# A graph layer over a dense adjacency: banks on 2048-byte starts, residual rows bank by bank, the emptying split, the first tiles rounded in parts, engine programs without loops

## What is computed

```python
h_in = jnp.maximum(_layernorm(x, axis=-1), 0.0)        # x is 10000 x 128
h = item_feat @ W_item.T + b_item                      # 10000 x 128
b = h_in @ W_user.T + b_user                           # 10000 x 128
return x + jax.nn.relu(adj @ h + b)                    # adj is 10000 x 10000
```

## Time and profile before

| | |
|---|---|
| median of three runs | 1132.15 us |
| the profiled execution | 1133.93 us |
| its span, first to last instruction | 1132.4 us |
| PE busy, matmuls | 1113.5 us, 98% |
| DVE busy | 974.1 us, 86% |
| ACT busy | 765.4 us, 68% |
| POOL busy | 23.0 us, 2% |
| DMA traffic | 421.44 MB, mean 372 GB/s |
| chain that ended last | PE 84%, DVE 6%, DMA 5% |

### The profile page before, as it was taken

How to read it: one execution, slowest core, us unless ns; L and a number is a source line. 1 busy time by engine, 2 the same in 40 slices (tenths; PEclk the granted TensorE clock), 3 DMA queues, 4 the chain that set the end, 5 groups by cost and what they waited for, 6 DMA issues and landing times.

```text
span 1132.4 us, 13599 instructions
## 1 busy us (share of the span) xinstructions
PE 1113.5 (98%) x4998; PEld 914.9 (81%) x4998; DVE 974.1 (86%) x683; ACT 765.4 (68%) x482; POOL 23.0 (2%) x47
## 2 busy tenths in 40 slices
PE   5999999999999999999999999999999999999998
PEld 4888888888888888878878888888788887887887
DVE  5899988889999878888988889888888898988887
ACT  4766766666666666676666666666666776666664
POOL 0000000001000000000000001000000010000000
PEclk9999999999999999999999999999999999999999
DMA  9999989999999999999999999999999999999994
GB/s 356 396 408 384 368 331 369 366 358 379 414 387 377 360 369 379 369 392 409 388 367 361 365 381 381 399 402 382 355 355 378 386 372 404 401 380 354 350 391 161
DMA packets 63378, 421.44 MB, mean 372 GB/s; under 512 B 7725, under 2 KB 9205, under 8 KB 63329
## 3 DMA queue, kind: packets, MB, share of 16 engines
q1 hardware_dynamic: 59984, 406.38, 92.6%
q0 software_dynamic: 3344, 14.34, 3.6%
HBM read 415.57 MB, written 5.12 MB: 372 GB/s over the span
## 4 chain that ended last, share of the span: by engine, by line
PE 84%; DVE 6%; DMA 5%; issue 3%; ACT 1%; SPq 1%; DVEq 0%; ACTq 0%
PE acc L536 27%; PE acc L529 27%; PE acc L531 26%; DMA a_ring<-in_adj_tiles 4%; DVE lo_ring L346 4%; ACT hi_ring L286 1%; PE acc L500 1%; PE acc L472 1%; DVE y L407 1%; PE acc L493 1%; DMA items<-in_item_t 1%; SPq L199 1%; PE acc L509 0%; SPq L192 0%; DVE stat L366 0%
## 5 line engine op out<-in xcount | busy, mean ns | idle before, releaser
L346 DVE TENSOR_TENSOR lo_ring<-a_ring,hi_ring 128x2000 fp32r<-128x2000 f32 x390 | 868.9, 2240 | 136.2 <-ACT hi_ring L286 135.8
L286 ACT CAST hi_ring<-a_ring 128x2000 fp32r<-128x2000 f32 x390 | 728.8, 1869 | 350.0 <-PE acc L536 324.0
L529 PE MATMUL acc<-hi_ring,h_lo 128*128 128x500 f32 x1560 | 617.9, 396 | 0.0
L536 PE MATMUL acc<-lo_ring,h_hi 128*128 128x500 f32 x1560 | 607.4, 389 | 3.9 <-DVE lo_ring L346 3.9
L531 PE MATMUL acc<-hi_ring,h_hi 128*128 128x500 f32 x1560 | 604.6, 388 | 0.0
L536 PEld LDWEIGHTS acc<-lo_ring,h_hi 128*128 128x128 f32 x1560 | 293.3, 188 | 67.8 <-DVE lo_ring L346 8.3
L529 PEld LDWEIGHTS acc<-hi_ring,h_lo 128*128 128x128 f32 x1560 | 293.5, 188 | 64.4 <-issue 8.5
L531 PEld LDWEIGHTS acc<-hi_ring,h_hi 128*128 128x128 f32 x1560 | 293.4, 188 | 62.0 <-issue 4.6
L472 PE MATMUL acc<-wi,items 128*128 128x128 f32 x156 | 23.9, 294 | 11.7 <-DMA items<-in_item_t 9.9
L472 PEld LDWEIGHTS acc<-wi,items 128*128 128x128 f32 x156 | 23.0, 206 | 13.9 <-issue 7.5
L351 DVE TENSOR_TENSOR h_full<-acc,bi 128x384 f32<-128x384 f32 x26 | 14.3, 552 | 11.5 <-PE acc L472 11.5
(11 more groups left out here) (27 smaller groups left out, 83.2 us busy)
## 6 DMA issues: line engine op xcount, KB each, us to landing
a_ring<-in_adj_tiles SPq DMA_DIRECT2D x390, 1000.0 KB, 7.0
rows<-in_x_rows POOLq DMA_DIRECT2D x20, 250.0 KB, 7.2
y<-in_x_t POOLq DMA_DIRECT2D x5, 1000.0 KB, 10.4
items<-in_item_t SPq DMA_DIRECT2D x12, 384.0 KB, 8.1
out_t<-y POOLq DMA_DIRECT2D x16, 250.0 KB, 5.5
out_t<-y SPq DMA_DIRECT2D x4, 250.0 KB, 2.1
a_rem<-in_adj_rem SPq DMA_DIRECT2D x20, 31.2 KB, 9.3
items<-in_item_t SPq DMA_DIRECT2D x2, 192.0 KB, 5.8
```

What stands on the lines that cost most here:

```text
L286: nc.scalar.copy(hi_ring[:, r, :], a_ring[:, s, 0:GROUP_W]).then_inc(hi_written, 1)
L346: nc.vector.tensor_tensor(lo_ring[:, r, :], a_ring[:, s, 0:GROUP_W], hi_ring[:, r, :], ALU.subtract).then_inc(lo_written[s], 1)
L529: nc.tensor.matmul(acc[k][:, 0:BANK_W], h_lo[:, c, :], hi_ring[:, r, cols], start=(c == 0), stop=False, skip_group_check=True)
L536: last = nc.tensor.matmul(acc[k][:, 0:BANK_W], h_hi[:, c, :], lo_ring[:, r, cols], start=False, stop=(c == CHUNKS - 1), skip_group_check=True)
```

## The change

- `hi_ring` and `lo_ring` get a pitch of 512 elements (2048 bytes) a bank. They are allocated early, behind three small tensors and a gap of 96 elements, so that the rings themselves begin on a multiple of 2048 bytes. `a_ring` now has banks of 500 and a slot of 2000 elements. In HBM the layout is as before.
- The x columns are loaded bank by bank, 0.25 MB each, the first when 9 tiles of a group are rounded and one more every 12.
- Emptying: two banks after the second tile of the next group, two after the third.
- The first three tiles are rounded and subtracted in four parts each. The first tile is loaded in four parts as well.
- `wi` and `bi` are loaded by ACT's queue. Only one trio of h stands ahead of the first tile; the next ones are made at tiles 1, 3 and 4. The first row load waits for two rounded tiles.
- PE makes 8 small products of the identity before the first trio and 6 behind it, into a bank that nobody reads.
- All loops of engines are written out, and waits on counts of zero fall away.

```diff
-        a_ring = sb("a_ring", [P, A_SLOTS, PITCH])
-        hi_ring = sb("hi_ring", [P, S_SLOTS, GROUP_W], F32R)
-        lo_ring = sb("lo_ring", [P, S_SLOTS, GROUP_W], F32R)
+        sb("gap", [P, RING_GAP])
+
+        hi_ring = sb("hi_ring", [P, S_SLOTS, ACC_BANKS, BANK_PITCH], F32R)
+        lo_ring = sb("lo_ring", [P, S_SLOTS, ACC_BANKS, BANK_PITCH], F32R)
...
+        a_ring = sb("a_ring", [P, A_SLOTS, ACC_BANKS, BANK_W])
...
-            sp.dma_start(wi[:, :], w_item_t).then_inc(w_item_loaded, 16)
             sp.dma_start(items[:, 0, 0:TRIO_W], item_t[:, 0:TRIO_W]).then_inc(item_first_loaded, 16)
-            sp.dma_start(bi[:, :], b_item_rows).then_inc(bias_loaded, 16)
-            load_tile(FREE, 0, 0)
+            for k in range(ACC_BANKS):
+                cols = slice(k * BANK_W, (k + 1) * BANK_W)
+                landed = part_loaded[k] if k < PARTS else a_loaded[0]
+                sp.dma_start(a_ring[:, 0, k, :], adj_tiles[0, :, cols]).then_inc(landed, 16)
             sp.dma_start(items[:, 0, TRIO_W:PIECE_W], item_t[:, TRIO_W:PIECE_W]).then_inc(item_loaded[0], 16)
-            load_tile(FREE, 1, 1)
+            load_tile(0, 1)
+            load_tile(0, 2)
             load_piece(1)
...
-            def load_x(g):
-                pool.dma_start(y[:, 0:GROUP_W], x_t[bass.ds(g, 1), :, :].rearrange("o p n -> (o p) n")).then_inc(x_loaded, 16)
+            def load_x(g, k):
+                pool.dma_start(y[:, k, :], x_t[g, :, k, :]).then_inc(x_loaded, 16)
+
+            pool.wait_ge(hi_written, 2)
+            load_rows(0, 0)
+            for g in range(GROUPS):
+                if g > 0:
+                    for k in range(ACC_BANKS):
+                        pool.wait_ge(y_ready[k], g)
+                        pool.dma_start(out_t[g - 1, :, k, :], y[:, k, :]).then_inc(stored, 16)
+
+                    pool.wait_ge(stored, g * (16 * ACC_BANKS))
+                for k in range(UNITS):
+                    if (g, k) != (GROUPS - 1, UNITS - 1):
+
+                        pool.wait_ge(centred_ready, g * UNITS + k + 1)
+                        load_rows(*divmod(g * UNITS + k + 1, UNITS))
+
+                    pool.wait_ge(hi_written, g * CHUNKS + X_AT + k * BODY)
+                    load_x(g, k)
...
+            def round_part(c, k):
+                s, r = c % A_SLOTS, c % S_SLOTS
+                if c == 0 and k < PARTS:
+                    act.wait_ge(part_loaded[k], 16)
+                else:
+                    tile_there(0, c)
+                nc.scalar.copy(hi_ring[:, r, k, 0:BANK_W], a_ring[:, s, k, :]).then_inc(part_hi if k < PARTS else hi_written, 1)
...
+                    elif c == AHEAD - 1:
+                        empty(g - 1, 0)
+                        empty(g - 1, 1)
+                    elif c == AHEAD:
+                        empty(g - 1, 2)
+                        empty(g - 1, 3)
...
+            pe.wait_ge(ident_set, 1)
+            warm(WARM_FIRST)
+            pe.wait_ge(w_item_loaded, 16)
+            h_trio(0)
+            warm(WARM_THEN)
```

More of the change, by code:

```diff
@@ L82 @@
 VAR_AT = 8
+X_AT = 9
 SQRT_AT = 11
@@ L88, with unit_at @@
 AHEAD = 2
-VECTOR_LOOP_AT = 2
-SCALAR_LOOP_AT = 6
+def unit_at(c, at):
+    k, rest = divmod(c - at, BODY)
+    return k if rest == 0 and 0 <= k < UNITS else None
 def graph_layer(nc, adj_tiles, adj_rem, ones_row, item_t, x_rows, x_t, w_item_t, b_item_rows, w_user_t, b_user, out_t):
@@ L142, in graph_layer @@
         a_loaded = [sem(f"a_loaded{s}") for s in range(A_SLOTS)]
+        part_loaded = [sem(f"part_loaded{k}") for k in range(PARTS)]
+        part_hi = sem("part_hi")
+        part_lo = sem("part_lo")
         rem_loaded = sem("rem_loaded")
@@ L274, in _ @@
         @block.scalar
         def _(act):
[L277 to L286 removed]
+            act.dma_start(wi[:, :], w_item_t).then_inc(w_item_loaded, 16)
@@ L332, in _, with h_rem_round, square @@
-            for g in range(1, GROUPS - 1):
-                group(g)
-                for c in range(AHEAD):
-                    round_hi(g + 1, c)
-            group(GROUPS - 1)
+            def h_rem_round():
+                act.wait_ge(h_rem_summed, 1)
+                for k in range(ACC_BANKS):
+                    row = k * ROWS_BLOCK
+                    nc.scalar.copy(h_rem[row:row + REM, :], h_full_rem[:, :]).then_inc(rem_set, 1)
+            def square(g, k):
+                act.wait_ge(centred_ready, g * UNITS + k + 1)
+                nc.scalar.activation(squares[:, :, :], centred[:, :, :], ACT.Square).then_inc(squares_ready, 1)
@@ L457, in _, with warm @@
+            for k in range(ACC_BANKS):
+                empty(GROUPS - 1, k)
         @block.tensor
         def _(pe):
+            def warm(times):
+                for _ in range(times):
+                    nc.tensor.matmul(warm_bank[0:ROW_T, 0:ROW_T], ident[:, :], ident[:, :], start=True, stop=True, skip_group_check=True)
             def h_trio(trio):
@@ L543, in _, with h_rem_product, turn_normed @@
-            pe.wait_ge(w_item_loaded, 16)
-            for trio in range(LEAD):
-                h_trio(trio)
-            pe.wait_ge(ident_set, 1)
-            for g in range(GROUPS):
-                group(g)
+            def h_rem_product():
+                pe.wait_ge(item_rem_loaded, 16)
+                nc.tensor.matmul(h_rem_bank[0:REM, 0:HID], items_rem[:, :], wi[:, :],
+                                 start=True, stop=True, skip_group_check=True).then_inc(h_rem_done, 1)
+            def turn_normed(g, k):
+                turned, n = turned_of(g), ROW_T
+                if g > 0 and k == 0:
+                    pe.wait_ge(y_ready[0], g)
+                pe.wait_ge(normed_ready, g * UNITS + k + 1)
+                for t in range(ROW_TILES):
+                    last = nc.tensor.transpose(turned[:, t * n:(t + 1) * n], normed[:, t, :], ident[:, :])
+                last.then_inc(turned_ready, 1)
```

437 lines of the change are left out of this document (214 added, 223 removed).

## The result

The changed kernel takes 1124.54 us (median of four runs, 1123.56 to 1124.76) where the kernel before, timed beside it, takes 1132.62 (1131.33 to 1133.58): a ratio of 0.9928, 95% interval 0.9911 to 0.9945. So it is faster by 8.1 us, inside the range and on the side that was forecast, but by only half of the 16 us. The profiled executions, 1133.93 and 1124.51 us, are 9.4 us apart, their spans 9.7.

A forecast was written before the change was run, and what follows sets the result against it. PE's matmul spacing was taken to bound nearly all the time. Start 3, residual rows 4.7, emptying 1.8 and bank alignment 7 made 16.5 us, less 0.5: 1132 - 16 = 1116 us, range 1070 to 1132.

The forecast's parts named there:

- What bounds the kernel: Whole kernel: the spacing of PE's matmul starts, 225.8 ns, bounds nearly all the time; DVE, ACT and DMA have slack.
- Start, 3 us: First tiles: fewer h products ahead and a row load moved let tile 3's third matmul start 3 us earlier.
- The two signs named: Expected in the changed kernel's trace: first main matmul near 9 us, tile 3's low part near 23.
- The lower bound, 1 us: Start of the kernel: the gain would be only 1 us if landings slip by 2 us.
- Warm-up, splitting, no loops, each 0: Identity products on PE, three tiles rounded in parts, and written-out engine loops were each to gain 0.
- Residual rows bank by bank, 4.7 us: Loads of x: 0.25 MB pieces remove PE waits for the low part in four places, 4.7 us, at least 2.
- Emptying split, 1.8 us: Four group boundaries: two banks emptied later let DVE's subtract begin 1.2 us sooner, removing waits of 1.8 us.
- Banks on 2048 bytes, 7 us: Moving operands of tile matmuls: aligned starts give every tile the better slot's 2.69 us instead of 2.71, 7 us.
- The second: Rival: the address cost each matmul up to 15 ns; spacing falls to 211 to 221 ns, 1053 to 1100 us; 24%.
- The third: Rival: equal bank starts make operand reads collide, 4 ns more a matmul, 1142 us; slower from 2 ns; 12%.
- The fourth: Rival: landings bind the start, another DVE step replaces the emptying, small x loads slow the queue; 1126 to 1132 us; 18%.

The follow-up runs named there:

- norm_later_0: Changed kernel with the layer norm steps and x loads of group 0 nine tiles later; 1122.11 us, ratio 0.9906.
- no_warm: Changed kernel without its 14 small products of the identity on PE; 1124.37 us, ratio 0.9927.
- align_unrolled: Kernel before with rings and banks aligned to 2048 bytes and the loops of SP, POOL, ACT and DVE written out; 1132.23 us, ratio 0.9996.
- split_six: Changed kernel with six tiles instead of three rounded and subtracted in parts; 1124.26 us, ratio 0.9931.
- x_at_once: Changed kernel with x loaded as one 1 MB DMA a group at its old place; 1129.51 us, ratio 0.9964.
- norm_later_1: Changed kernel with all layer norm steps of groups 1 to 4 two tiles later; 1123.23 us, ratio 0.9919.
- packed: Changed kernel with banks at 2000 bytes again and the rings' start modulo 2048 as in the kernel before; 1129.33 us, ratio 0.9963.
- align_layout: Kernel before with the changed kernel's whole SBUF layout, but its own loops, order, x load and emptying; 1129.94 us, ratio 0.9970.
- align_only: Kernel before with only hi_ring and lo_ring changed: banks 2048 bytes apart, rings on a multiple of 2048; 1132.40 us, ratio 0.9993.
- rings_behind: Changed kernel with a_ring allocated ahead of the gap and rings, banks still on multiples of 2048 bytes; 1126.85 us, ratio 0.9953.
- a_ring_pitch: Changed kernel with a slot of a_ring at 2048 elements instead of 2000; 1126.03 us, ratio 0.9944.

## Why the prediction missed by half

The side, the range and the kinds of gain came out; the sum did not. The steps that failed are three of its terms. The start and the residual rows were added up although both are bound by the same landings: up to tile 78 they were to give 3 and 1.8 us and gave 1.3. The emptying was checked one tile ahead only: 0.4 instead of 1.8. And the spacing was taken from the better slot for all tiles: 4.9 instead of 7.

**What bounds the kernel**: right. PE's starts account for the whole difference.

**Start, 3 us**: 1.4. The two signs named came, tile 0 near 9 (8.09) and tile 3's low part near 23 (21.50). The step stopped at tile 3. It said that tiles cannot be had before they land, and then credited the gain at tile 3 as if the later tiles were not landing-bound as well; tile 6 landed at 28.3 in both. The lower bound, 1 us, was the better value, though not for the reason given there, late landings: tile 3 landed at 17.3, where the step had 19.0. `norm_later_0` shows what else lay behind it: without the layer norm's centring ahead of tile 5's subtract, tile 6 starts 2.1 us earlier, while it lands only 0.3 us earlier.

**Warm-up, splitting, no loops, each 0**: right for the warm-up and the loops (`no_warm`, `align_unrolled`). More splitting brings nothing (`split_six`); the first three split tiles were not undone alone.

**Residual rows bank by bank, 4.7 us**: about 2.9 of it came, the share of groups 1 to 4. The 1.8 us of group 0 hardly did: the wait at tile 13 is nearly as long as in the earlier trace rows, although of x only a quarter was loaded by then (issued at 35.90, landed at 42.71 us) and tile 13 itself landed at 49.5 instead of 51.1. PE was earlier by as much and met the same wait, for a late landing with the layer norm's steps on DVE on top. So the split load did act in group 0, but what it gave was the start's gain over again: `x_at_once` loses that gain by tile 78. Two terms of the sum were one. `norm_later_0` takes the wait away, by moving the layer norm and the x loads together, which does not tell the two apart. The term is also conditional: taken out of the changed kernel the same edit costs 4 to 5 us (`x_at_once`). That a faster PE leaves less time to catch up would explain it and is not shown.

**Emptying split, 1.8 us**: 0.3 to 0.4. The step looked one tile on ("Next is tile 81") and found 0.2 us of slack. It had to add up DVE's work up to the sixth tile, where the centring comes on top. Four waits of 0.16 to 0.36 us, and about 0.1 behind each, replace the old ones, and `norm_later_1` takes them away by moving the layer norm, the centring with it.

**Banks on 2048 bytes, 7 us**: 5.3 in groups 1 to 4, less 0.4 in group 0, where spacing rose from 226.0 to 226.5. The size was near, the reason was not. It took the tile of the better slot, 2.69 us, for all; no tile has it. There are tiles of 2.68 and of 2.72, and 2.69 is their mixture. The layout is what brings it (`packed`, `align_layout`), but not the start of the banks alone (`align_only`, `rings_behind`). That the size came near is luck: the prediction knew of slots, not of two patterns.

Against the forecast, 1.6 us are missing at the start, 1.8 in the rows of group 0, 1.4 in the emptying and 2.1 in the spacing, 6.9 of the 16.5; the 9.6 that are left are the 9.7 of the two spans. The median fell by 1.3 us less than the profiled execution did (8.1 against 9.4), since the profiled execution of the kernel before lay above its median.

**The rivals.** The second (211 to 221 ns) is out: in no run did twelve distances in a row come below 223 ns in the mean. By the Trainium skill, "TensorE: Matmul & The Clock Gate", section "Back-to-back issue gap", whose formula for the isolated gap is N / 2.4 + 2.5 ns, it would have been 210.8 ns; no run here agrees. The third (slower from 2 ns a matmul) is out as well: the slow pattern of 226.7 ns is only 0.8 ns above the spacing of before. The fourth was true in two of its three parts: landings bind at the start, and another DVE step took the emptying's place.

**Still open**: why a layout favours one pattern. Every edit that changed the share of fast tiles also moved the buffers that PE reads between tiles, and the traces point at these. A run that moves them alone was not made. What of the interruption picks the pattern was not found.

## What to carry to other kernels

When a stall on a helper engine is taken away, add up that engine's work until its slack has paid the lateness back, not only to the next tile; and when the first tiles start sooner, ask when the later ones land. The gain at a tile is only kept if everything behind it can move too. An edit of SBUF addresses that is timed alone, without its surroundings, may show nothing, so test it also by taking it out of the finished kernel. Such an edit also moves every buffer allocated behind it; list them before you name a cause.

## What was not expected of the hardware

- PE's spacing for 500 columns with a weight load each has two steady patterns, 223.3 and 226.7 ns in the mean. Which one holds changes only at interruptions, and its share depends on addresses, even when those of the tile matmuls' own operands stay (`a_ring_pitch`, 1 ns).
- In `no_warm`, eight distances in a row of 500 columns are 0.42 us each, the pace of the lower of the two clock levels (1.2 GHz), while the row of granted clock shows 1.00 for 7 to 12 us. By the Trainium skill, "TensorE: Matmul & The Clock Gate", section "Back-to-back issue gap", the cold distance is N / 1.2, 417 ns for 500 columns, and this trace agrees. The granted clock in the rows does not show this stretch, the distances of starts do.
- DMA throughput of the one core reached 429 GB/s at 8 to 12 us of the changed kernel (426 in a window of the earlier trace rows), and 375 in the mean. The window's row has the columns of the earlier trace rows:

```profile
8.00:12.00 4.00, 3.62 (x18) 3.00 (x18) 2.19 (x5) 1.57 (x3) 0.00 (x0) 1.00 1.02 429
```
